# Cross-attention: the eight units' probabilities summed on VectorE alone, the two halves folded in TensorE's denominator product

## The reference

```python
x = x + xattn(layernorm(x), ctx, Wq, Wk, Wv, Wo)      # 16 heads of 32
Q = (query @ Wq.T).reshape(B, 128, 16, 32)
K = (context @ Wk.T).reshape(B, 2048, 16, 32)
V = (context @ Wv.T).reshape(B, 2048, 16, 32)
attn = softmax(einsum('bqhd,bkhd->bhqk', Q, K) / sqrt(32))
out = einsum('bhqk,bkhd->bqhd', attn, V).reshape(B, 128, 512) @ Wo.T
```

## Time and profile before

| what | us |
|---|---|
| median of 3 runs (lowest, highest) | 1845.63 (1844.68, 1847.39) |
| the profiled execution, its own time | 1844.61 |
| its span, first to last instruction | 1843.1 |
| PE busy, share of the span | 1654.4 (90%) |
| DVE busy | 1174.1 (64%) |
| ACT busy | 772.6 (42%) |
| GpSimd busy | 442.4 (24%) |

### The profile page before, as it was taken

The page is one execution under the profiler, slowest core; times in us unless marked ns, Lnnn a source line. Parts: engine busy times, 40 slices in busy tenths (PEclk is TensorE's granted clock), DMA queues, the critical chain, the costliest instruction groups (busy, mean ns, idle before and its releaser), DMA issues. The chain is left out here.

```text
span 1843.1 us, 42551 instructions
## 1 busy us (share of the span) xinstructions
PE 1654.4 (90%) x17522; PEld 1139.0 (62%) x17522; DVE 1174.1 (64%) x1343; ACT 772.6 (42%) x967; POOL 442.4 (24%) x379
## 2 busy tenths in 40 slices
PE   6899899999999999999998996948319999999996
PEld 4656566666666666666666664826216777777774
DVE  5668467567567567667667564686755566565654
ACT  4345236335345345354354343156614344344330
POOL 3223222222312312222223274330060100000022
PEclk9999999999999999999999998868659999999998
DMA  6523243243233332332332343400365654454523
GB/s 244 137 69 106 63 115 81 50 110 81 60 100 81 74 99 70 77 103 63 89 90 64 69 133 75 143 1 3 127 192 168 210 188 160 165 187 143 210 81 117
DMA packets 102285, 202.65 MB, mean 110 GB/s; under 512 B 25767, under 2 KB 25767, under 8 KB 102012
## 3 DMA queue, kind: packets, MB, share of 16 engines
q1 hardware_dynamic: 91820, 170.74, 32.1%
q0 software_dynamic: 10320, 29.67, 5.1%
HBM read 128.36 MB, written 19.05 MB: 80 GB/s over the span
## 5 line engine op out<-in xcount | busy, mean ns | idle before, releaser
L566 DVE TENSOR_REDUCE mx<-sc 128x4 f32<-128x2048 f32 x128 | 293.3, 2292 | 88.7 <-PE sc L788 88.1
L427 ACT ACTIVATE probs<-sc 128x1024 f32<-128x1024 f32 x256 | 248.2, 1024 | 72.7 <-PE sc L821 72.0
L390 ACT ACTIVATE v_sb<-proj 128x512 f32<-128x512 f32 x128 | 76.4, 597 | 367.9 <-PE proj L749 367.9
L329 POOL TENSOR_TENSOR acc_g<-probs 128x1024 f32<-128x1024 f32 x31 | 73.1, 2357 | 513.5 <-ACT probs L427 513.4
L588 DVE TENSOR_TENSOR acc_v<-acc_v,probs 128x1024 f32<-128x1024 f32 x93 | 129.5, 1392 | 88.2 <-ACT probs L427 85.6
L1033 DVE SCALAR_TENSOR_TENSOR w_lo<-stage_w,w_hi 128x2048 f16<-128x2048 f32 x64 | 144.5, 2289 | 47.5 <-ACT w_hi L1027 47.5
L749 PE MATMUL proj<-w_hi,ctx_hi 128*128 128x256 f16 x1024 | 161.0, 281 | 15.3 <-ACT ctx_hi L379 12.4
L749 PE MATMUL proj<-w_lo,ctx_hi 128*128 128x256 f16 x1024 | 159.7, 280 | 1.2 <-DVE w_lo L522 1.2
L749 PE MATMUL proj<-w_hi,ctx_lo 128*128 128x256 f16 x1024 | 159.8, 280 | 0.2 <-DVE ctx_lo L528 0.2
L534 DVE SCALAR_TENSOR_TENSOR k_lo<-proj,k_hi 128x512 f16<-128x512 f32 x128 | 87.9, 687 | 106.2 <-ACT k_hi L399 105.4
L1937 ACT ACTIVATE hf<-ph 128x321 f32<-128x321 f32 x128 | 56.4, 441 | 226.5 <-PE ph L2107 201.8
(11 more groups left out here) (308 smaller groups left out, 2790.8 us busy)
## 6 DMA issues: line engine op xcount, KB each, us to landing
stage_w<-in_w SPq DMA_DIRECT2D x64, 1024.0 KB, 5.9
stage<-in_ctxT SPq DMA_DIRECT2D x64, 512.0 KB, 4.3
ks<-k_hi SPq DMA_DIRECT2D x256, 128.0 KB, 2.4
ks<-k_lo SPq DMA_DIRECT2D x128, 128.0 KB, 2.4
wq_f<-in_wiT POOLq DMA_DIRECT2D x24, 256.0 KB, 4.2
xbuf<-zeros SPq DMA_DIRECT2D x20, 256.0 KB
xg<-xbuf POOLq DMA_DIRECT2D x14, 256.0 KB, 5.5
obuf<-o_sb POOLq DMA_DIRECT2D x14, 256.0 KB, 2.5
```

Of the source, the lines that this page charges most:

```text
L390: act.activation(v_sb[:, half, 2 * n:2 * n + 2, :], proj[where % 2][:, :].rearrange("p (c d) -> p c d", c=2), ACT.Copy, scale=1.0 / WSCALE ...
L427: act.activation(probs[:, u % 4, :], unit_scores(u), ACT.Exp, scale=1.0 / sqrt(HD)).then_inc(e_ready, 1)
L566: dve.tensor_reduce(mx[:, :, kb], sc[:, :, :], AX.X, ALU.max).then_inc(m_read, 1)
```

## The change

All seven additions of a group are made on DVE: `add_probs(b, g, n)` adds unit n+1 to `acc_v`, for n from 0 to 6. In `body`, part 0 makes the first, part 1 makes three (units 2, 3 and 4), part 2 one (unit 5) and part 3 two (units 6 and 7). `acc_g` and its four GpSimd instructions a group are gone, and with them GpSimd's loop over batches 1 to 6. The denominators' product reads both halves of `acc_v` and accumulates them in PSUM: eight matmuls instead of four. ACT's waits before it overwrites a `probs` buffer, and PE's before the product, count DVE's additions alone. The diff, cut to its core:

```diff
-                        at = 16 * b + 4 * g
-                        if not (last and g == 3):
-                            gp.wait_ge(e_ready, e + 4)
-                            if not (isinstance(b, int) and b == 0 and g == 0):
-                                gp.wait_ge(group_done, 4 * b + g)
-                            gp.tensor_tensor(acc_g[:, :], probs[:, 2, :], probs[:, 3, :], ALU.add).then_inc(sum_g, 1)
-                            if first_batch(b):
-                                load_weight(4 * g + 2, 0)
-                            gp.wait_ge(e_ready, e + 8)
...
-                            gp.tensor_tensor(acc_g[:, 0:512], acc_g[:, 0:512], acc_g[:, 512:1024], ALU.add).then_inc(sum_g, 1)
+                        if first_batch(b):
+                            load_weight(4 * g + 2, 0)
                         if first_batch(b):
                             load_weight(4 * g + 3, 0)
...
-                with nc.Fori(1, B - 1, engines=(mybir.EngineType.Pool,), hint_back_edge=True) as b:
-                    body(b, False)
...
-                        who, val = {0: (sum_v, k - 2), 1: (sum_v, k - 1), 2: (sum_v, k), 3: (sum_g, k - 2),
-                                    4: (sum_v, k + 1), 5: (sum_v, k + 1), 6: (sum_g, k + 1), 7: (sum_g, k + 1)}[u]
+                        added = ADDS * (4 * b + g) + (-3, -2, -1, 0, 1, 1, 2, 3)[u]
...
-                            act.wait_ge(who, val)
+                            act.wait_ge(sum_v, added)
...
+                def add_probs(b, g, n):
+
+                    dve.wait_ge(e_ready, 32 * b + UNITS * g + n + 2)
+                    if n == 0:
...
+                        dve.wait_ge(sum_v, ADDS * (4 * b + g) + n)
+                        dve.tensor_tensor(acc_v[:, :], acc_v[:, :], probs[:, (n + 1) % 4, :], ALU.add).then_inc(sum_v, 1)
...
-                                add_probs(b, g, part)
+                                for n in ((0,), (1, 2, 3), (4,), (5, 6))[part]:
+                                    add_probs(b, g, n)
...
-                    pe.wait_ge(sum_g, 16 * b + 4 * g + 4)
-                    for j in range(GH):
-                        last = pe.matmul(po[HD * j:HD * j + HD, T:2 * T], ones[:, 0:HD], acc_g[:, P * j:P * j + P],
-                                         start=True, stop=True, tile_position=(0, HD * j))
+                    pe.wait_ge(sum_v, ADDS * (4 * b + g + 1))
+                    for i in range(2):
+                        for j in range(GH):
+                            last = pe.matmul(po[HD * j:HD * j + HD, T:2 * T], ones[:, 0:HD],
+                                             acc_v[:, 512 * i + P * j:512 * i + P * j + P],
+                                             start=i == 0, stop=i == 1, tile_position=(0, HD * j))
```

More of the change, by code:

```diff
@@ L94, in cross_attention @@
         acc_v = sb("acc_v", [P, 1024], f32)
-        acc_g = sb("acc_g", [P, 1024], f32)
         mx = sb("mx", [P, GH, KB], f32)
@@ L152, in cross_attention @@
         sum_v = sem("sum_v")
-        sum_g = sem("sum_g")
         group_done = sem("group_done")
@@ L183, in cross_attention @@
         LEAD = 1
+        ADDS = UNITS - 1
         def weight_piece(n):
@@ L318, in body @@
                     for g in range(G):
-                        e = 32 * b + UNITS * g
                         if first_batch(b) and g:
@@ L322, in body @@
                             load_weight(4 * g + 1, 0)
-                        at = 16 * b + 4 * g
-                        if not (last and g == 3):
-                            gp.wait_ge(e_ready, e + 4)
-                            if not (isinstance(b, int) and b == 0 and g == 0):
-                                gp.wait_ge(group_done, 4 * b + g)
-                            gp.tensor_tensor(acc_g[:, :], probs[:, 2, :], probs[:, 3, :], ALU.add).then_inc(sum_g, 1)
-                            if first_batch(b):
-                                load_weight(4 * g + 2, 0)
-                            gp.wait_ge(e_ready, e + 8)
-                            gp.wait_ge(sum_g, at + 1)
-                            gp.tensor_tensor(acc_g[:, :], acc_g[:, :], probs[:, 3, :], ALU.add).then_inc(sum_g, 1)
-                            gp.wait_ge(sum_v, at + 4)
-                            gp.wait_ge(sum_g, at + 2)
-                            gp.tensor_tensor(acc_g[:, :], acc_g[:, :], acc_v[:, :], ALU.add).then_inc(sum_g, 1)
-                            gp.wait_ge(sum_g, at + 3)
-                            gp.tensor_tensor(acc_g[:, 0:512], acc_g[:, 0:512], acc_g[:, 512:1024], ALU.add).then_inc(sum_g, 1)
+                        if first_batch(b):
+                            load_weight(4 * g + 2, 0)
                         if first_batch(b):
@@ L420, in exp @@
                         act.wait_ge(pv_done, e - 3)
-                        k = 4 * g + 16 * b
-                        who, val = {0: (sum_v, k - 2), 1: (sum_v, k - 1), 2: (sum_v, k), 3: (sum_g, k - 2),
-                                    4: (sum_v, k + 1), 5: (sum_v, k + 1), 6: (sum_g, k + 1), 7: (sum_g, k + 1)}[u]
+                        added = ADDS * (4 * b + g) + (-3, -2, -1, 0, 1, 1, 2, 3)[u]
                         if not (isinstance(b, int) and b == B - 1 and g == 3 and u >= 4):
-                            act.wait_ge(who, val)
+                            act.wait_ge(sum_v, added)
                     act.activation(probs[:, u % 4, :], unit_scores(u), ACT.Exp, scale=1.0 / sqrt(HD)).then_inc(e_ready, 1)
@@ L576, in maxima_to_diag @@
                                       ALU.mult).then_inc(diag_ready, 1)
-                def add_probs(b, g, part):
-                    e = 32 * b + UNITS * g
-                    dve.wait_ge(e_ready, e + (2, 5, 6, 7)[part])
-                    if part == 0:
+                def add_probs(b, g, n):
+                    dve.wait_ge(e_ready, 32 * b + UNITS * g + n + 2)
+                    if n == 0:
                         if not (isinstance(b, int) and b == 0 and g == 0):
@@ L586, in add_probs @@
                     else:
-                        dve.wait_ge(sum_v, 16 * b + 4 * g + part)
-                        dve.tensor_tensor(acc_v[:, :], acc_v[:, :], probs[:, (0, 0, 1, 2)[part], :],
-                                          ALU.add).then_inc(sum_v, 1)
+                        dve.wait_ge(sum_v, ADDS * (4 * b + g) + n)
+                        dve.tensor_tensor(acc_v[:, :], acc_v[:, :], probs[:, (n + 1) % 4, :], ALU.add).then_inc(sum_v, 1)
                 def finish_group(b, g, steps):
```

## The result

The changed kernel takes 1853.53 us (median of 6 runs, 1851.31 to 1855.52), the kernel before 1844.53 us beside it on the same chip (6 runs, 1841.15 to 1847.39): a ratio of 1.0049, with a 95% interval of 1.0035 to 1.0063. It is slower by about 9 us. The forecast was 1846.4 us, within 0.2% of before; the time lies above its range of 1841.0 to 1852.5.

What follows compares the result with a forecast made beforehand. PE was taken to bound the kernel, at 90% of the span; 7.6 + 2.6 + 2.5 + 1.0 - 4.1 - 7.7 - 1.1 = +0.8 us on 1845.6 gave 1846.4 us, range 1841.0 to 1852.5.

Steps and rivals of the forecast that it cites:

- rival B: End of batch 0: nothing given back, the -7.7 us lost; +8.5 us, 1854.1 us in all; chance 0.09.
- PE's added half: Denominators' product: four more matmuls in 30 groups that count, 0.25 us a group; +7.6 us.
- Rival A: Denominators' product: PE's second four matmuls cost 0.36 us like the first; +5.7 us, 1851.3 us; chance 0.17.
- DVE's chain outside group 2: Groups 0, 1 and 3: added additions fit DVE's idle time, 0.3 us left, next maximum not later; 0.
- DVE's chain in group 2: Loop, group 2: three more additions, 3.99 us, less 3.55 of slow instructions gone; wait 2.47, +2.6 us over six batches.
- Batch 0: Ends of groups 1, 2 and 3: waits become 1.4, 4.0 and 1.4 us; -4.1, +2.5 and -7.7 us.
- Batch 7, quantiser +1.0 and wait -1.1: Batch 7: GpSimd's early quantiser holds up DVE additions, +1.0 us; PE's wait at group 1's end goes, -1.1.
- The clock: Loop batches: PE's low-clock spells after waits stay at five of six; 0, with +1.7 or -8.4 us possible.
- rival C: Loop: three of five low-clock spells after waits vanish, 5.1 us off; -4.3 us, 1841.3 us; chance 0.14.

Runs made afterwards that it cites:

- before_place: Kernel before plus 96 redundant waits (48 instructions) where PE idles in batch 0, shifting its loop; 1854.39 us against 1842.20, ratio 1.0078.
- after_pad: Changed kernel plus 80 redundant waits (40 instructions) in PE's prologue, shifting its loop; 1840.90 us against 1842.16 for the kernel before, ratio 0.9990.
- before_pad: Kernel before plus 122 redundant waits (61 instructions) in PE's prologue, shifting its loop; 1847.31 us against 1842.16, ratio 1.0025.

## Why the prediction was wrong

Two steps failed. The first is in the forecast's first paragraph: "Everywhere else in the loop PE is the bound and every instruction added to it counts in full." It counted the added instructions by their busy time only; where they put the loop in the program was no term of the sum and no rival, and it measured +5.1 us net. The second is the term for batch 7: it priced the early quantiser by its two operations that hold up DVE, +1.0, and put its DMAs at nothing; the group measured +6.1. By the table above, either alone would have left the time inside the range; both took it out. That rival B names nearly the same time, 1854.1 us, is a coincidence: what it describes did not happen. The profile had shown the hint: one stall of 2.9 us on "issue" just behind the loop (at 1013 us), which the forecast leaves out: the window of rows 1 ends at 1009.

- **PE's added half, +7.6.** Measured 0.22 us a group, +6.5. Timeline of PE in batch 3, the product and what follows, answering to rows 3:

```profile
545.36 0.64 PE L837 MATMUL po<-acc_v,ones 128*32 128x128 f32 x16
545.94 1.04 PE L741 MATMUL proj<-ctx_hi,w_hi 128*128 128x512 f16 x4
```

  From start to start 0.58 us, against 0.36 before, so the price was the one of equal matmuls in a row. Rival A, 0.36 for the second half, is out. The rule that it quotes of the Trainium skill (page "TensorE: Matmul & The Clock Gate", section "The mechanism"), that a weight load overlaps running matmuls only when it goes to another group of rows, is not borne out here: all use the same rows, and the eight added loads, some 0.11 us each in the trace, run beside matmuls and fit into the added 0.22 us.
- **Its instructions, priced at nothing beyond that.** +10.1 us in five stalls and -5.0 at the loop's end. Shown by before_place (the stall without the work) and after_pad (the work without the stall). The Trainium skill, on the page "Runtime: NRT & Kernel Launch", section "Instruction fetch mechanics", says that instructions come in blocks of 256 (16 KiB), that crossing into the next is mostly hidden, and that a jump to a target not at hand has to fetch it first. The packets of 16.4 KB agree. The traces differ on what is dear: in the changed kernel the jump costs 0.2 us and the crossing behind it 1.9. By that rule of the Trainium skill there would be a stall at every jump, in both kernels, or none; it gives no reason why 48 instructions more should bring one.
- **DVE's chain outside group 2, 0.** Right: no new wait at the ends of groups 0 and 1 in the loop. At the end of group 1 in batch 3 DVE's idle time ahead of the last split of K fell from 1.64 to 0.21 us, where the forecast had 0.3 left.
- **DVE's chain in group 2, +2.6.** The mechanism was right and the size a little high: the wait is 2.2 us and not 2.47, +0.8 in six batches, since a dependent addition starts 1.25 us after the one before and not 1.33. The slow instructions of 2.63 and 3.38 us are both gone, as the forecast had it from rows 8; they were GpSimd's doing. In the kernel before, each ended 1.08 us after an addition of GpSimd's that had started earlier. Timeline of POOL there:

```profile
555.89 2.37 POOL L329 TENSOR_TENSOR acc_g<-probs 128x1024 f32<-128x1024 f32 x1 [18.59 <-ACT probs L427]
562.65 3.11 POOL L334 TENSOR_TENSOR acc_g<-acc_g,probs 128x1024 f32<-128x1024 f32 x1 [4.39 <-ACT probs L427]
```

- **Batch 0.** End of group 1: wait 1.37 against 1.4 forecast, -4.2 against -4.1. End of group 2: 3.95 against 4.0, +3.5 against +2.5. End of group 3: the weight piece is not waited for any more, -5.7 against -7.7; the wait is 2.04 and not 1.4, and PE is slow after it (0.61 us for the first scores). Rival B, nothing back at this place, is out. DVE's last two reductions of the batch, without a wait between them:

```profile
187.48 1.27 DVE L670 TENSOR_REDUCE wq_max<-wq_f 128x1 f32<-128x512 f32 x2
```

- **Batch 7, quantiser +1.0 and wait -1.1.** The forecast named its operations and let it go by the locks on DVE. Those are there (1.47 and 1.66 us for additions of 1.23). It did not price what the quantiser also issues, eight DMAs in 17 us beside the stacked K. Measured +6.1 in group 0; pacing gives 5.9 of it back. The wait of 1.09 us at the end of group 1 stayed, 1.15: the addition that GpSimd had held up is no longer slow, but one more stands in its place. DVE there, before and after:

```profile
1080.61 2.69 DVE L588 TENSOR_TENSOR acc_v<-acc_v,probs 128x1024 f32<-128x1024 f32 x1
...
1092.74 2.55 DVE L566 TENSOR_TENSOR acc_v<-acc_v,probs 128x1024 f32<-128x1024 f32 x2 [1.68 <-issue]
```

- **The clock, 0.** In the loop -3.3 us, one low-clock spell fewer in batches 1, 2 and 4 and one more in batch 3, with waits of nearly one length. Nothing in the runs ties it to a step of the change, so its cause is open; rival C, three spells fewer, held in part.

The sum of the forecast's own terms as measured is 6.5 + 0.8 - 4.2 + 3.5 - 5.7 + 1.1 = +2.0, against +0.8: those terms alone would have kept it in the range. What was left out, +5.1 for the code's place and +6.1 in batch 7, group 0, made the result. With the clock's -3.3 and +1.1 of other rows of the table that is the span's growth. That the clock took off 3.3 us is luck that hid part of the error. after_pad, without the five stalls and with part of the loss in batch 7, stands at 0.9990.

## What to carry over

When an edit changes the number of instructions on the engine that bounds the kernel, look at the stalls on "issue" near its loop's start and end before and after, and shift the code to see what the layout alone is worth: here up to 12 us (0.8%) with no work changed, more than the 9 us between the two kernels. When a queue is freed from a wait, price every transfer that now starts sooner against those that a busier engine waits for. And where an in-order engine waits for data with ready work behind it, move the waiting instruction: that was worth 13 us here.

## What the runs showed of the hardware

- PE can stall 1.2 to 2.1 us some 22 instructions behind a loop's jump back, at every jump, and 2.4 to 2.9 us once some 10 behind its end, depending on where the loop lies in the program. With such stalls the instruction queue moved 135 packets, without them 129 or 130 (before_pad and after_pad too).
- Redundant waits are not free on PE: 220 of them, two to an instruction, took 10.1 us.
- DMAs of 128 KB from SyncE's queue landed in 2.4 to 2.5 us when alone and in 5.2 to 7.7 us (medians) beside transfers of GpSimd's queue; in batch 7 the two queues took 45.5% and 39.5% of the DMA engines.
- GpSimd held up DVE's two-input instructions by up to 2.2 us (3.38 for 1.23). The Trainium skill's page "SBUF — State Buffer", section "Who interferes with whom", says that a VectorE instruction with two inputs in SBUF contends with a GpSimd instruction that reads SBUF, and with GpSimd's additions gone the trace agrees: in group 2 the split takes 1.23 us and the additions 1.25 from start to start, none longer. A TENSOR_SCALAR with one input, on seven numbers, took 1.12 us beside GpSimd's fold and 0.27 in the changed kernel.
- A run of dependent additions of 1024 columns on DVE starts one every 1.25 us (5.00 / 4).
